# Where VectorE's inverse of the 16-row base blocks stands among its other work, in the attention part of a hybrid layer stack

## The reference

```python
mixed = silu(causal_conv4(x @ w_qkv)); z = x @ w_z
q, k, v = split(mixed)                 # 16 key heads, 32 value heads of 128; two value heads share a key head
beta, g = sigmoid(x @ w_b), -exp(A_log) * softplus(x @ w_a + dt_bias)
q, k = l2norm(q) * 128**-0.5, l2norm(k)
for t in range(1024):                  # per batch and value head; state is 128 x 128
    state = state * exp(g[t])
    state += outer(k[t], (v[t] - k[t] @ state) * beta[t])
    out[t] = q[t] @ state
x = x + (norm_w * rms_normed(out) * silu(z)) @ w_out
```

## Time and profile before

| what | value |
|---|---|
| median of 3 runs | 4165.66 us (4164.44 to 4167.02) |
| the profiled execution's own time | 4168.05 us |
| its span, first to last instruction | 4166.1 us |
| PE busy (page, part 1) | 3997.3 us, 96% |
| DVE, ACT, POOL busy | 3196.9 us (77%), 2592.6 us (62%), 958.8 us (23%) |
| mean granted TensorE clock | 0.991 of full speed |

### The profile page before, as it was taken

The page is one execution under the profiler, slowest core; times in us unless marked ns, Lnnn a source line. Parts: engine busy times, 40 slices in busy tenths (PEclk is TensorE's granted clock), DMA queues, the critical chain, the costliest instruction groups (busy, mean ns, idle before and its releaser), DMA issues. The chain is left out here.

```text
span 4166.1 us, 83038 instructions
## 1 busy us (share of the span) xinstructions
PE 3997.3 (96%) x29437; PEld 2282.0 (55%) x29437; DVE 3196.9 (77%) x8334; ACT 2592.6 (62%) x6087; POOL 958.8 (23%) x1110
## 2 busy tenths in 40 slices
PE   7999999999999999999999999998899999999999
PEld 4555556556555555566565555555444444444444
DVE  4777887787787777877778877777447989898940
ACT  3566676666666666666666666666445656574643
POOL 1224333234333243333333333332100000000000
PEclk9999999999999999999999999999999999999999
DMA  3223334333433433343334333334304545454510
GB/s 131 83 72 84 87 86 90 85 80 85 92 77 85 120 82 85 90 86 85 81 87 92 75 87 85 82 80 97 83 1 132 164 148 168 147 175 153 183 57 10
DMA packets 290733, 402.99 MB, mean 97 GB/s; under 512 B 25774, under 2 KB 125362, under 8 KB 290258
## 3 DMA queue, kind: packets, MB, share of 16 engines
q1 hardware_dynamic: 253458, 330.57, 26.1%
q0 software_dynamic: 36864, 67.13, 12.0%
HBM read 288.56 MB, written 113.25 MB: 96 GB/s over the span
## 5 line engine op out<-in xcount | busy, mean ns | idle before, releaser
L676 PE MATMUL bank<-x_blocks,rows_b 128*128 128x512 f32 x1536 | 713.0, 597 | 0.9 <-ACT partial L914 0.9
L1306 DVE SCALAR_TENSOR_TENSOR conv<-raw,conv_w,conv 128x1024 f32<-128x1024 f32 x384 | 522.7, 1361 | 61.9 <-ACT conv L1008 56.8
L676 PE MATMUL bank<-x_blocks,w_pair 128*128 128x512 f32 x1152 | 549.9, 605 | 14.8 <-DVE x_blocks L1277 4.5
L831 PE MATMUL bank<-w_out_unit,oT 128*128 128x512 f32 x1008 | 491.4, 610 | 0.9 <-ACT out_stage L931 0.9
L676 PEld LDWEIGHTS bank<-x_blocks,rows_b 128*128 128x128 f32 x1536 | 274.9, 190 | 249.1 <-issue 231.3
L1662 PE MATMUL bank<-xnT_f,w_gu 128*128 128x512 f32 x704 | 324.5, 605 | 1.2 <-ACT xnT_f L2161 0.9
L1291 DVE SCALAR_TENSOR_TENSOR oT<-bank,norm_w,z 128x256 f32<-128x256 f32 x252 | 119.2, 473 | 261.4 <-PE bank L761 260.3
L676 PEld LDWEIGHTS bank<-x_blocks,w_pair 128*128 128x128 f32 x1152 | 206.8, 193 | 205.5 <-issue 169.5
L2231 ACT ACTIVATE step_decay<-dt,rate 128x512 f32<-128x512 f32 x256 | 183.4, 720 | 217.1 <-DVE h L2340 215.0
L1681 PE MATMUL bank<-w_down,hidden 128*128 128x512 f32 x704 | 316.9, 594 | 1.7 <-DVE x_blocks L1740 1.7
L1671 PE MATMUL bank<-xnT_f,w_gu 128*128 128x512 f32 x704 | 316.8, 593 | 0.5 <-DVE hidden L1702 0.5
(11 more groups left out here) (270 smaller groups left out, 8360.8 us busy)
## 6 DMA issues: line engine op xcount, KB each, us to landing
x_after<-out_stage POOLq DMA_DIRECT2D x256, 256.0 KB, 4.2
rows_b<-bc_rows SPq DMA_DIRECT2D x256, 256.0 KB, 3.6
rows_c<-bc_rows SPq DMA_DIRECT2D x256, 256.0 KB, 3.7
w_pair<-in_w_qkv SPq DMA_DIRECT2D x128, 256.0 KB, 3.9
decay<-gc_rows SPq DMA_DIRECT2D x64, 512.0 KB, 5.0
z<-z_rows SPq DMA_DIRECT2D x64, 512.0 KB, 5.1
z_rows<-x_blocks SPq DMA_DIRECT2D x96, 256.0 KB, 5.8
w_pair<-in_w_z SPq DMA_DIRECT2D x64, 256.0 KB, 3.3
```

Of the source, the lines that this page charges most:

```text
L676: made = e.matmul(bank[:, :], weight[:, j, :], part(0, m)[:, j, :], start=j == 0 and m in (1, 5), stop=j == 1, skip_group_check=True)
L831: made = e.matmul(out_rows(N, t)[:, :], turned_to(N, t)[:, r, :], w_out[:, N % 2, r, :], start=r == 0, stop=r == REP - 1)
L1306: e.scalar_tensor_tensor(acc, raw[:, i, tap:tap + T], conv_w[:, tap, col:col + 1], acc, ALU.mult, ALU.add).then_inc(on["conv"], 1)
```

## The change

No instruction is added, removed or resized. DVE's program is put in another order; the order on PE, ACT and POOL is unchanged.

- Half 0 and half 1: section 0 of the base inverse moves to the front part of its slot (offset 10 or 14), ahead of the product read at place "a" and of `gate_out`.
- The columns are cut differently. 1 to 3 go to the front part of offset 11 or 15, also ahead of place "a" and `gate_out`; 4 to 6 and 7 to 10 stand together where 1 to 6 stood.
- Columns 11 to 14 with L1194 go, for half 0, to the front part of offset 12; for half 1, from the end of offset 16 to offset 17, right behind that slot's `resid`.
- The decay subtraction of half 1 goes from ahead of `turn_base` to behind `gate_out` in offset 9.

```diff
                 for j in range(1, BASE - 1):
-                    if section == (1 if j < 7 else 2 if j < 11 else 3):
+                    if section == (1 if j < 4 else 2 if j < 7 else 3 if j < 11 else 4):
...
-                if section == 3:
+                if section == 4:
...
+            def subtract(slot, a):
+                n = unit_at_only(slot, 8 + a)
+                if n is not None:
+                    if a == 0:
...
+                        e.tensor_tensor(col_beta[:, :, :], gc_beta[:, n // HK, heads, :], norm, ALU.add).then_inc(
+                            on["col_beta"], 1)
+                    e.wait_ge(on["chunk_exp"], 2 * n + a + 1)
+                    e.wait_ge(on["col_beta"], n + 1)
+                    dec = decay_half(n, a)
+                    col = col_beta[:, :, HALF * a:HALF * (a + 1)].unsqueeze(3).broadcast_to([P, REP, HALF, P])
+                    e.tensor_tensor(dec, dec, col, ALU.subtract).then_inc(on["decay_sub"], 1)
...
+                n = unit_at_only(slot, 17)
+                if n is not None:
+                    base_inverse(n, 1, 4)
                 for a in range(2):
                     n = unit_at_only(slot, 9 + 4 * a)
                     if n is not None:
                         evict_pair(n, a, 0)
-                for a in range(2):
-                    n = unit_at_only(slot, 8 + a)
...
+                subtract(slot, 0)
                 for a in range(2):
                     n = unit_at_only(slot, INVERSE + 4 * a)
                     if n is not None:
                         e.wait_ge(on["mask"], 2 * n + a + 1)
                         turn_base()
+                for a in range(2):
+                    for section, at in ((0, 10 + 4 * a), (1, 11 + 4 * a), (4, 12)):
+                        n = unit_at_only(slot, at)
+                        if n is not None and (section < 4 or a == 0):
+                            base_inverse(n, a, section)
                 read_at(slot, "a")
                 gate_out(slot)
-                n = unit_at_only(slot, 10)
-                if n is not None:
-                    base_inverse(n, 0, 0)
+                subtract(slot, 1)
                 convolve(slot, (2, 1))
                 for a in range(2):
                     n = unit_at_only(slot, 11 + 4 * a)
                     if n is not None:
-                        base_inverse(n, a, 1)
+                        base_inverse(n, a, 2)
+                        base_inverse(n, a, 3)
...
-                    n = unit_at_only(slot, 10 + 4 * a)
-                    if n is not None and a == 1:
-                        base_inverse(n, a, 0)
-                    n = unit_at_only(slot, 11 + 4 * a)
-                    if n is not None:
-                        base_inverse(n, a, 2)
-                    n = unit_at_only(slot, 12 + 4 * a)
-                    if n is not None:
-                        base_inverse(n, a, 3)
```

More of the change, by code:

```diff
@@ L1293, in gate_out @@
                             on["oT_copy"], 1)
+            def subtract(slot, a):
+                n = unit_at_only(slot, 8 + a)
+                if n is not None:
+                    if a == 0:
+                        if n in (0, HK):
+                            e.wait_ge(on["gates"], n // HK + 1)
+                        e.wait_ge(on["ln"], n + 1)
+                        if n > 0:
+                            e.wait_ge(on["decay_sub"], 2 * n)
+                        norm = ln_norm[:, n % 3, K, :].unsqueeze(1).broadcast_to([P, REP, NC])
+                        heads = slice(REP * (n % HK), REP * (n % HK + 1))
+                        e.tensor_tensor(col_beta[:, :, :], gc_beta[:, n // HK, heads, :], norm, ALU.add).then_inc(
[5 more added lines that the diff above has]
+                    e.tensor_tensor(dec, dec, col, ALU.subtract).then_inc(on["decay_sub"], 1)
             def convolve(slot, taps):
```

## The result

| | before | changed |
|---|---|---|
| median (4 runs each) | 4165.05 us (4163.18 to 4167.02) | 4210.02 us (4208.08 to 4211.46) |
| ratio, 95% interval | | 1.0108 (1.009 to 1.0125) |
| profiled execution: time / span | 4168.05 / 4166.1 us | 4208.08 / 4206.1 us |
| period of a unit, unit 13 | 88.25 us | 89.25 us |

The change makes the kernel 1.1% slower: 45 us by the medians, 40.0 by the two profiled spans. The direction and most of the places were as forecast, the size was not: 4196 us was given, with a range of 4170 to 4210, and 4210.02 lies at its very end, just outside.

What follows compares the result with a forecast made beforehand. PE, busy 96% of the span, was taken as the bound. Per unit +0.15 + 0.80 + 0 = 0.95 us, over 30 units 28.5, plus 2.0 in slot 265: span 4166.1 to 4196.6, forecast 4196 us, range 4170 to 4210.

Steps and rivals of the forecast that it cites:

- part 1: Slot 121, `resid` ahead of columns 11 to 14: L780's 1.02 us wait moves to L605, 0.08 us won.
- part 2: Slot 119, columns 4 to 10 ahead of the `z_extra` read: 0.25 us late a unit, bounds 0.2 and 0.54.
- The chain: Slot 121, from the end of `ks` through `resid`, columns and POOL's mask to L605: 5.98 us.
- both waits: PE waits at L605 for POOL's mask, some 1.2 us, and at L676 for the `z_extra` read, about 0.5 us.
- Part 3: Slot 122, section 0 ahead of the read at place "a": L1008 and L617 late, +0.80 us a unit.
- the meeting with POOL: Slot 122, section 0's tensor-tensor instructions meet POOL's L1460: 0.50 us added; without it, +0.28 us a unit.
- Part 4: Half 0's last columns early in offset 12: `resid` wait goes, L608 still waits for ACT; gain 0, bound -0.15.
- Part 5: Slot 121, decay subtraction behind `gate_out`: cost 0, unless POOL's L1498 is there first.
- the 2.0 kept: Slot 265, without products to hide the longer chain to L605: +2.4 us, of which 2.0 was kept.

Runs made afterwards that it cites:

- Experiment 6: Changed kernel with columns 7 to 10 of both halves back at the end of offsets 11 and 15: 4199.68 us, ratio 1.0079.
- experiment 8: Kernel before with one move alone, half 1's columns 11 to 14 behind `resid` in offset 17: 4182.77 us, ratio 1.004.
- experiments 1 and 2: 1: changed kernel with half 0's section 0 back behind `gate_out`, 4189.14 us; 2: changed kernel with POOL's L1460 waiting for that section, 4196.35 us.
- experiment 4: Changed kernel with half 0's columns 11 to 14 back at the end of offset 12: 4202.19 us, ratio 1.0084.
- experiment 7: Changed kernel with half 1's decay subtraction back ahead of `turn_base`: 4209.96 us, ratio 1.011.
- spread: Kernel before with only half 1's section 0 and both halves' columns 1 to 3 moved early: 4149.93 us, ratio 0.9965.
- half1_back: Changed kernel with half 1's columns 11 to 14 back at the end of offset 16, ahead of `resid`: 4194.27 us, ratio 1.0067.
- spread_split: `spread_act` with half 0's columns 11 and 12 early in offset 12, the rest at its end: 4119.95 us, ratio 0.9891.
- spread_read: `spread_split` with ACT's copy L910 between the two Silus of offset 5: 4092.39 us, ratio 0.9824.
- spread_act: `spread` with ACT's `off` copy L1068 moved ahead of the Silu of `z`: 4117.79 us, ratio 0.9891.

## Why the prediction was right in direction and too small

**Parts 1 and 2** right in their places and, partly by luck, in their sum: predicted +0.15 us a unit, measured -1.38 + 1.06 + 0.42 = +0.10. The chain (5.92 us for 5.98) and both waits are where they were put. Experiment 6, without the late read, shows the two terms: part 1 gains 0.23 us (-1.28 + 1.05) and not 0.08, of which 0.10 is that `ks` in slot 121 takes 0.60 us and no longer 0.70; and part 2 costs 0.42 less the 0.10 that comes back in slot k=0, so 0.32 and not 0.25, within its bounds. The two misses cancel. And part 1's number stands on the columns that part 2 moves; alone it costs 0.60 (experiment 8).

**Part 3** right: +0.80 predicted, 0.72 measured, of which the meeting with POOL 0.48 for 0.50 (experiments 1 and 2).

**Part 4** was mis-sized: "gain 0", measured a loss of 0.20 us a unit; with this part alone taken back the kernel takes 4202 us and not 4210 (experiment 4). The step that failed is the last sentence: "DVE has the 4 us of the removed columns for that". These columns had stood behind `state` and now stand ahead of it, where DVE had 3.0 us of idle time and took 3.9 us of columns into it. What it has left there is the time by which `state` is done ahead of `ks`: 1.32 us, 1.27 without the hand-over of 0.05. The taps start 0.20 us later behind the columns and take 1.17 us longer, together 1.37, so `ks` is 0.10 us late and its first group 0.10 longer. The 0.8 us named were right for what the mask does to the first tap (0.83). Not seen was the weight sum that POOL has queued behind the mask, 0.34 more on the second tap. By these rows the mask alone would still have fitted; no run shows that by itself.

The wait of 0.8 us that was forecast at L608 is there in two pieces, 0.46 us at L676 for L910 and 0.25 at L608. That the second chain takes up what the first gives back was right.

**Part 5** right: 0 (experiment 7). The subtraction was 0.08 us ahead of POOL's L1498, for the 0.1 counted, so this order was nearly the other one.

**The sum.** The steady part was forecast at 0.95 us a unit and is 1.02: the 0.20 of part 4 is nearly hidden by parts 1 to 3, which came out 0.13 lower. In the span the forecast was 30.5 us and 40.0 were measured. Of the 9.5 missing, the steady part has 1.1, the part ahead of slot 24 has 6.7, and the end, from slot 256 on, 1.7 (3.7 for the 2.0 kept).

The end is made otherwise than forecast. L605 in slot 265 waits 4.49 us and comes 5.91 us behind `ks`, as the forecast's chain of 5.98 had it, but by the last L780 only 1.0 us more is lost than at slot 264, and the layers behind give 1.4 back. The 4.1 us are lost in slots 256 to 263:

```profile
2924.69 0.42 DVE L1425 TENSOR_TENSOR o<-bank,q_state 128x256 f32<-128x256 f32 x1
2925.14 0.31 ACT L1127 ACTIVATE k_scaled<-o 128x128 f32<-128x128 f32 x1 [2.15 <-DVE o L1425]
...
2925.86 0.58 ACT L931 COPY out_stage<-bank 128x512 f32<-128x512 f32 x1
...
2926.50 0.69 PE L761 MATMUL bank<-ident,o 128*128 128x128 f32 x2 [4.04 <-ACT out_stage L931]
```

In slot 263 no product is left, and there DVE's `o` stands behind columns 4 to 10. ACT's squares wait for `o`, ACT's `out_stage` copy stands behind them, and PE's L761 waits for that copy, 4.04 us. With columns 7 to 10 back it is 1.8. Part 2 was priced in slots where products hide this, and not in the last ones. Behind the wait of 4.04 us PE's granted clock is 0.50 from 2926 to 2930 us, the lower of its two levels (1.2 GHz), and the four L831 in this slot take 3.05 us; before, with 1.79 us of waiting there, the clock in this slot is 1.00 and they take 1.88. What the lower clock costs was not separated: in experiment 6, where the wait is 1.79 us too, they take 2.96.

The part ahead of slot 24 was forecast at 0 and is 6.7 us. Some 3 us of it are there by slot 8 (its subtraction starts at 110.30 us, before at 107.20), up to where the order on DVE is the same; the start of the first matmul alone (12.96 or 13.32 us) and the first slots differ like that between runs. In the twelve kernels of the experiments slot 24 is between 2.3 us earlier and 7.4 later than before. But they fall into two groups: the seven that keep most of the change have it 3.4 to 7.4 us later, the five built on the kernel before between 2.3 earlier and 1.7 later. So a part of the 6.7 is likely the change's own; which instruction makes it stays open.

The rest of the 14 us between 4196 and 4210, some 4.5, is between span and median: the median of the changed kernel lies 3.9 us above its profiled span, and the forecast put it 0.4 below, as in the kernel before, and rounded down.

## What to carry to other kernels

A wait is worth only the distance to the second chain that ends there; here two of DVE's ended 0.06 us apart, and behind them ACT's. Work is moved for nothing only into idle time of its own engine that ends before something is waited for, so the moves into DVE's idle time alone (spread) gained where the whole change lost. When an instruction comes earlier, list what other engines have queued behind it, and look where that will run. And price each edit once more in the first and the last round, where the work that covers it is missing.

## What the runs showed of the hardware

**DVE and POOL in SBUF.** The same two instructions met in both orders. In the changed kernel DVE's subtraction started 0.08 us ahead of POOL's L1498: DVE took 1.21 us and POOL 2.88. In `half1_back` POOL started 0.27 us ahead: POOL took 1.90 us and DVE 2.71. The first loses nothing, the second waits about for the first's end. This is the rule of the Trainium skill's page "SBUF — State Buffer" (section "Who interferes with whom"), by which the shared port pair is an exclusive lock. By it DVE would have lost 1.90 - 0.27 = 1.63 us, and it lost 1.50; POOL 1.21 - 0.08 = 1.13 us, and it lost 0.98. The trace agrees but for 0.13 to 0.15 us, as in the section 0 meeting (0.49 us for 0.64). For the two taps of slot 124 it is 0.20: 0.83 us lost for 1.02 of meeting the mask, 0.34 for 0.55 of meeting the weight sum.

**A wait can cost more than its bracket.** In slot k=5 `spread_split` shows a wait of 0.47 us at L676, and `spread_read`, without it, has 0.73 us less in that slot. The 0.26 us more are the 0.16 by which PE otherwise starts ahead of the end before, and the 0.10 by which the first group behind a wait is longer (1.98 for 1.88 us, and 0.71 for 0.61 at L780). So the `resid` wait of 1.02 us was worth 1.25 (slot k=0 in `spread`). It is not so for every group: at L608, whose matmuls are 32 wide, a wait of 0.62 us went in `spread_act` and the slot got only 0.69 shorter. My estimates for `spread_act` and `spread_read` counted brackets alone, and both came out too small; for `spread_act` the larger part of what was missing is slot k=5, which also got 0.14 us shorter, and some 4 us ahead of slot 24.
